# A graph network on one core: sixteen small products of each batch dealt out among its columns

## The chip, the cores and the metric

One NeuronCore of a Trainium2 chip runs the whole program in one launch. The metric is the device time in microseconds, the median over the runs. The core has a matrix engine (TensorE; PE in the rows, its weight loads PEld), VectorE (DVE), ScalarE (ACT), GpSimd (POOL) and SyncE (SP), each with its own instruction stream; they meet only at semaphores.

## The reference, cut to what matters

The program is a chain of four graph layers over 3,750 nodes and 123,750 edges (`src`, `dst`, with attributes): a relational convolution, a weighted one, two attention layers and a tensor product. All of them sum messages per destination node:

```
msg = Hr[src, etype] * norm
agg = jax.ops.segment_sum(msg, dst, num_segments=N)
```

The kernel sorts the edges by destination once, so that every later layer walks them in that order. The change lies in this sort.

## The kernel before, in words

The sort has two parts. `count_edges` counts the edges of each node and so finds each node's first free slot. `place_edges` then takes the edges in 121 batches (`SBATCHES`) of 8 columns (`SB`) of 128 edges, finds for each edge the slot that it goes to, and GpSimd scatters the 80-byte records to DRAM, one indirect DMA for each column (line 717).

A destination is split in a low part (7 bits, `lo`) and a high part (`hi`, 30 values, `BLKS`). A table of counters over (low, high) is a 128 x 30 array. An edge's slot is the sum of three things, all summed by TensorE into `own[j][:, k, 0:BLKS]` for batch buffer `j` (the batch's number modulo 2) and column `k`:

- `earlier` x `hot_hi` (line 667): edges of the same column that stand earlier and go to the same node;
- `hot_lo_t` x `taken_in` (line 671): what the earlier columns of the batch have taken. `taken[j]` counts it (line 673, a product of the one-hots `hot_lo` and `hot_hi` that adds up over the columns, its end raises `added`), and ScalarE copies it as f16 to `taken_in` after each column but the last (line 704, raises `taken_copied`);
- `hot_lo_t` x `high` and `hot_lo_t` x `low` (lines 677 to 682, the rows call them L680): the nodes' next free slots at the start of the batch, as two f16 digits. These are 2 x 8 = 16 products of 128x128 by 128x30. They stand behind the eighth column, in one burst; ahead of them is a wait on `based`, and the last raises `owned`.

VectorE, for each batch `b` in this order: `find_base(b)` waits for all `added` of batch b-1, adds `taken` to the base and splits it into `high` and `low` (lines 612 to 615, the last raises `based`); `pick_slots(b-1)` waits for `owned` of batch b-1, picks the slot of each edge (lines 620 to 624) and makes row numbers (lines 232 to 235, the last raises `rows_ready`); `find_hots(b+1)` makes the one-hots of the next batch (lines 596 to 601, the last raises `hot`). TensorE begins batch b after `hot` of batch b. GpSimd waits for `rows_ready` of a batch and sends its 8 indirect DMAs. The one-hots, `own` and `taken` have two buffers, `rows` four.

Beside this, 240 chunks of the first layer's table are made: up to two for each batch, a 128x128 by 128x512 f32 product behind the columns 2 and 5 (line 656), copied out by ScalarE (line 695) and stored by SyncE. SyncE also loads `lo_wide`, 256 KB for each batch (line 571), as soon as `hot` frees its buffer.

Of the kernel before, what the change touches and what calls it, by code (L numbers as in the profile page):

```python
# [31 lines left out]
BLKS = -(-N // P)  # L32
# [10 lines left out]
SB = 8  # L43
# [201 lines left out]
def sort_edges(env, inp, dst, records, relation_layers, weights_dram, table):  # L245

    nc = env.nc
    with ExitStack() as ctx:
        sb, ps = stage_memory(nc, ctx, "sort")
        parts = {
            "recs": sb("recs", [P, EC, REC], F32),
            "lo": sb("lo", [P, EC], F16),
            "hi": sb("hi", [P, EC], F16),
            "lo_f32": sb("lo_f32", [P, EC], F32),
            "node_row": sb("node_row", [P, BLKS], I32),
            "node_rec": sb("node_rec", [P, BLKS, REC], F32),  # L260
            "base": sb("base", [P, 2, BLKS], F32),
            "space": sb("space", [P, D * D // 2], F32),
        }
        lo_rows = nc.dram_tensor("lo_rows", (EC, P), F16, kind="Internal").ap()
        count_edges(env, inp, dst, records, relation_layers, weights_dram, lo_rows, parts)
        place_edges(env, records, lo_rows, table, parts)
# [249 lines left out]
def place_edges(env, records, lo_rows, table, parts):  # L516
# [14 lines left out]
    with ExitStack() as ctx:  # L531
# [3 lines left out]
        hot_lo_t = sb("hot_lo_t", [P, 2, SB, P], F16)  # L535
        earlier = sb("earlier", [P, 2, SB, P], F16)
        hot_hi = sb("hot_hi", [P, 2, SB, BLKS], F16)
        high = sb("high", [P, 2, BLKS], F16)
        low = sb("low", [P, 2, BLKS], F16)
# [9 lines left out]
        own = [ps(f"own{j}", [P, SB, 64], F32) for j in range(2)]  # L549
# [4 lines left out]
        s = {n: env.sig(f"place_{n}").sem for n in (  # L554
            "hot", "based", "added", "taken_copied", "owned", "rows_ready", "self_written", "x_turned", "x_ready",
            "table_made", "table_out")}
# [3 lines left out]
        table_rows = table.rearrange("(n h r) f -> n h (r f)", h=2, r=REL // 2)  # L560
        block = ctx.enter_context(nc.Block(no_gpsimd_drain=True))

        def table_chunks(b):
            return range(max(0, (b - made_at) * per_batch), min(BLKS * chunks, (b - made_at + 1) * per_batch))

        @block.sync
        def _(sp):
            def load_lo(b):
                if b >= lo_bufs:
                    sp.wait_ge(s["hot"], b - lo_bufs + 1)  # L570
                sp.dma_start(lo_wide[:, b % lo_bufs, :, :].rearrange("p k e -> p (k e)"),
                             lo_rows[b * SB:(b + 1) * SB, :].rearrange("k e -> (k e)").partition_broadcast(P)
                             ).then_inc(lo_in[b % lo_bufs], 16)

            def store(half):
                sp.wait_ge(s["table_out"], 4 * half + 4)
                sp.dma_start(table_rows[half // 2 * P:(half // 2 + 1) * P, half % 2, :], made[half % 3]).then_inc(stored[half % 3], 16)

            half = 0
            for b in range(SBATCHES):  # L580
                load_lo(b)
                while half < halves and 4 * half + 4 <= max(0, (b - lo_bufs - made_at) * per_batch):
                    store(half)
                    half += 1
            for last in range(half, halves):
                store(last)
            for j in range(3):
                sp.wait_ge(stored[j], 16 * len(range(j, halves, 3)))
# [54 lines left out]
        @block.tensor  # L643
        def _(pe):
            def turn_x(blk):
                if blk:
                    pe.wait_ge(s["x_ready"], blk)
                pe.transpose(turn_ps[:, 0:P], env.x[:, blk, :], env.ident[:, :]).then_inc(s["x_turned"], 1)

            def make_table(n):  # L650
                blk, c = n // chunks, n % chunks
                if c == 0:
                    pe.wait_ge(s["x_ready"], blk + 1)
                if n >= 2:
                    pe.wait_ge(s["table_out"], n - 1)
                pe.matmul(out_ps[n % 2][:, :], x_t[:, blk % 2, :], weights[:, c * cols:(c + 1) * cols], start=True,
                          stop=True).then_inc(s["table_made"], 1)
                if c == 0 and blk + 1 < BLKS:
                    turn_x(blk + 1)

            turn_x(0)
            for b in range(SBATCHES):
                j = b % 2
                left = list(table_chunks(b))
                pe.wait_ge(s["hot"], b + 1)
                for k in range(SB):
                    pe.matmul(own[j][:, k, 0:BLKS], earlier[:, j, k, :], hot_hi[:, j, k, :], start=k == 0, stop=True,
                              skip_group_check=True)
                    if k:
                        pe.wait_ge(s["taken_copied"], b * (SB - 1) + k)  # L670
                        pe.matmul(own[j][:, k, 0:BLKS], hot_lo_t[:, j, k, :], taken_in[:, k % 2, :], start=False, stop=True,  # L671
                                  skip_group_check=True)
                    pe.matmul(taken[j][:, 0:BLKS], hot_lo[:, j, k, :], hot_hi[:, j, k, :], start=k == 0, stop=True,
                              skip_group_check=True).then_inc(s["added"], 1)
                    if left and k in (2, 5):
                        make_table(left.pop(0))
                pe.wait_ge(s["based"], b + 1)
                for k in range(SB):
                    for digit in (high, low):
                        mm = pe.matmul(own[j][:, k, 0:BLKS], hot_lo_t[:, j, k, :], digit[:, j, :], start=False, stop=True,  # L680
                                       skip_group_check=True)
                mm.then_inc(s["owned"], 1)

        @block.scalar
        def _(act):
# [1864 lines left out]
```

## Time and profile before

| what | value |
|---|---|
| median of 3 runs | 11323.88 us (11316.15 to 11333.89) |
| the profiled execution, its time | 11423.42 us |
| its span, first to last instruction | 11421.7 us |
| mean granted TensorE clock | 0.623 of full speed |
| PE / PEld / DVE / ACT / POOL busy | 62% / 46% / 51% / 27% / 58% of the span |
| indirect DMAs of the placing stage (line 717) | 968, from 166.3 to 1681.8 us |

The profiled execution is one run with the profiler on; its time stands above the median of the plain runs. Shares are means over stages with different limits, so they don't say what the placing stage waits for. In the rows below a start is in microseconds from the first instruction; "idle before" is the time in which that engine did nothing ahead of the instruction, with what released it. A PE row's start is when the product was issued to the array; when it was done shows in the instruction that waits for its semaphore.

### The profile page before, as it was taken

What the parts mean: (1) busy time and instruction counts of PE and PEld (TensorE: products, weight loads), DVE (VectorE), ACT (ScalarE), POOL (GpSimd) and SP (SyncE); (2) the same over time, 40 slices, a digit from 0 to 9 for tenths busy, and PEclk for the clock granted to TensorE, in tenths of its full rate; (3) what the DMA queues carried; (4) which work ended last, traced back from release to release, by engine and by line L of the source; (5) the groups of instructions that cost most, each with busy time, mean ns of one, the idle gap of its engine ahead of it and who ended that gap; (6) DMA issues with size and microseconds to landing.
All of it is one profiled execution on the core that took longest, in us unless ns stands there. A gap on an engine that the chain in (4) does not pass through costs nothing. (4 is left out here: it accounts for less than half of the span.)

```text
span 11421.7 us, 173435 instructions
## 1 busy us (share of the span) xinstructions
PE 7099.6 (62%) x35190; PEld 5300.1 (46%) x35190; DVE 5879.9 (51%) x20916; ACT 3126.7 (27%) x10511; POOL 6581.8 (58%) x6970
## 2 busy tenths in 40 slices
PE   5444444433383333358888767777577777788888
PEld 3222223333332323334444356666566666777777
DVE  5555543333333333345544456666566666677776
ACT  2111110000020000000000044444344444677776
POOL 3666666666515655656666566666466665455554
PEclk5555555555585555555555556666666656899999
DMA  3222223111151111111111111111111111211111
GB/s 99 72 69 69 72 73 80 46 45 44 42 227 44 44 44 42 44 45 46 46 46 45 45 48 49 49 48 49 44 48 48 48 48 43 75 41 41 41 41 40
DMA packets 312728, 637.47 MB, mean 56 GB/s; under 512 B 138402, under 2 KB 181541, under 8 KB 300200
## 3 DMA queue, kind: packets, MB, share of 16 engines
q0 software_dynamic: 222080, 416.54, 14.1%
q1 hardware_dynamic: 81444, 212.40, 5.4%
q14 instruction: 579, 4.74, 0.1%
q8 instruction: 141, 2.31, 0.1%
q10 hardware_dynamic: 8484, 1.48, 0.1%
HBM read 479.02 MB, written 150.90 MB: 55 GB/s over the span
## 5 line engine op out<-in xcount | busy, mean ns | idle before, releaser
L1185 POOL DMA_INDIRECT relsum_rows<-relation_table,tab_idx x1950 | 1842.2, 945 | 1422.7 <-issue 484.9
L1241 PE MATMUL relsum_sums<-relsum_hot,relsum_rows 128*128 128x128 f32 x3900 | 1109.3, 449 | 1452.5 <-issue 797.1
L1241 PEld LDWEIGHTS relsum_sums<-relsum_hot,relsum_rows 128*128 128x128 f32 x3900 | 915.6, 307 | 1638.9 <-issue 1600.7
L1053 POOL DMA_INDIRECT conv_rows<-tensor_table,src_idx x997 | 939.9, 943 | 750.9 <-PE conv_sums L2360 357.2
L1053 POOL DMA_INDIRECT gat2sum_rows<-gat_table,src_idx x997 | 942.8, 946 | 587.7 <-PE gat2sum_sums L1971 308.6
L1053 POOL DMA_INDIRECT gat1sum_rows<-gat_table,src_idx x997 | 941.6, 944 | 582.3 <-PE gat1sum_sums L1971 255.1
L717 POOL DMA_INDIRECT records<-sort_recs,place_rows x968 | 926.4, 957 | 595.0 <-DVE place_rows L235 325.1
L1185 POOL DMA_INDIRECT gcnsum_rows<-x_table,src_idx x985 | 935.0, 949 | 562.6 <-PE gcnsum_sums L1241 259.1
L1969 PE MATMUL gat1sum_sums<-gat1sum_hot,gat1sum_scaled 128*128 128x128 f32 x1994 | 686.1, 443 | 413.0 <-DVE gat1sum_scaled L1898 332.9
L1197 DVE TENSOR_SCALAR relsum_hot<-iota_row,dst_rel,w 128x128 f32<-128x128 f32 x1994 | 722.8, 365 | 423.5 <-issue 421.4
L1969 PE MATMUL gat2sum_sums<-gat2sum_hot,gat2sum_scaled 128*128 128x128 f32 x1994 | 671.5, 436 | 432.3 <-DVE gat2sum_scaled L1898 302.0
L1241 PE MATMUL gcnsum_sums<-gcnsum_hot,gcnsum_rows 128*128 128x128 f32 x1970 | 781.9, 500 | 0.0
L2238 ACT ACTIVATE conv_rows_attr<-conv_rows,conv_rec 128x64 f32<-128x64 f32 x2991 | 737.8, 333 | 13.4 <-SPq L2197 12.8
L1969 PEld LDWEIGHTS gat2sum_sums<-gat2sum_hot,gat2sum_scaled 128*128 128x128 f32 x1994 | 469.3, 291 | 565.4 <-issue 509.7
L1969 PEld LDWEIGHTS gat1sum_sums<-gat1sum_hot,gat1sum_scaled 128*128 128x128 f32 x1994 | 470.3, 292 | 555.9 <-DVE gat1sum_scaled L1898 429.9
L1218 DVE TENSOR_TENSOR acc<-acc,relsum_sums 128x128 f32 x997 | 287.4, 288 | 823.7 <-PE relsum_sums L1241 376.5
L1240 PE MATMUL gcnsum_sums<-gcnsum_hot,ones 128*1 128x128 f32 x1994 | 581.1, 394 | 199.7 <-issue 139.3
L1218 DVE TENSOR_TENSOR acc<-acc,gcnsum_sums 128x256 f32 x997 | 419.6, 421 | 553.4 <-PE gcnsum_sums L1241 515.8
L671 PE MATMUL place_own<-place_taken_in,place_hot_lo_t 128*128 128x30 f16 x847 | 170.4, 201 | 841.5 <-ACT place_taken_in L704 675.5
L1241 PEld LDWEIGHTS gcnsum_sums<-gcnsum_hot,gcnsum_rows 128*128 128x128 f32 x1970 | 492.5, 310 | 421.2 <-issue 421.2
L1218 DVE TENSOR_TENSOR rel_acc<-rel_acc,relsum_sums 128x128 f32 x997 | 287.2, 288 | 725.3 <-remote 462.8
L2283 DVE TENSOR_TENSOR tp_acc<-tp_acc,conv_sums 128x384 f32 x999 | 550.0, 551 | 170.6 <-PE conv_sums L2360 119.0
(410 smaller groups left out, 15931.9 us busy)
## 6 DMA issues: line engine op xcount, KB each, us to landing
relation_table<-table_row SPq DMA_DIRECT2D x30, 2048.0 KB, 6.3
relsum_rows_SP<-relation_table SPq DMA_DIRECT2D x2816, 0.5 KB
relsum_rows_ACT<-relation_table ACTq DMA_DIRECT2D x2816, 0.5 KB
relation_table<-sort_space SPq DMA_DIRECT2D x40, 1024.0 KB
relsum_rows<-relation_table,tab_idx POOLq DMA_INDIRECT x1950
place_lo_wide<-lo_rows SPq DMA_DIRECT2D x121, 256.0 KB
gcnsum_rows_SP<-x_table SPq DMA_DIRECT2D x1536, 0.5 KB
relation_table<-place_extra SPq DMA_DIRECT2D x20, 1024.0 KB
```

Source lines behind the costliest of these rows:

```text
L671: pe.matmul(own[j][:, k, 0:BLKS], hot_lo_t[:, j, k, :], taken_in[:, k % 2, :], start=False, stop=True, skip_group_check=True)
L717: pool.indirect_dma_start(records, bass.IndirectOffsetOnAxis(ap=rows[:, b % row_bufs, k:k + 1], axis=0), recs[:, b * SB + k, :], None).the ...
L1053: pool.indirect_dma_start(bufs[:, t % depth, :], None, table, bass.IndirectOffsetOnAxis(ap=idx[:, t:t + 1], axis=0)).then_inc(landed[t % l ...
L1185: pool.indirect_dma_start(rows[:, t % depth, :], None, table, bass.IndirectOffsetOnAxis(ap=idx[:, t:t + 1], axis=0)).then_inc(landed[t % d ...
L1197: dve.tensor_scalar(hot[:, t % HOTS, :], env.iota_row[:, :], env.dst_rel[:, t:t + 1], weight[:, t:t + 1], ALU.is_equal, ALU.mult).then_inc ...
L1218: dve.tensor_tensor(window, window, sums[t % banks][:, 0:parts * P].rearrange("p (a n) -> p a n", a=parts), ALU.add).then_inc(s["added"], 1)
L1240: pe.matmul(bank[0:1, P:2 * P], env.ones[:, 0:1], hot[:, t % HOTS, :], start=True, stop=True)
L1241: pe.matmul(bank[:, 0:P], tile_rows, hot[:, t % HOTS, :], start=True, stop=True).then_inc(s["multiplied"], 1)
L1969: pe.matmul(bank[:, 0, 0:P], scaled[:, j, :, :].rearrange("p h c -> p (h c)"), hot[:, k, :], start=True, stop=True)
L2238: last = act.activation(rows_attr[:, k % 8, m, :].rearrange("p (i u) -> p i u", i=2), by_block[:, 0:m + 2:m + 1, :], ACT.Identity, scale=a ...
L2283: dve.tensor_tensor(window, window, sums[(k - 2) % 4][:, 0:3 * P].rearrange("p (a n) -> p a n", a=3), ALU.add).then_inc(s["added"], 1)
```

## The change

The burst behind the eighth column goes. Behind column `k` TensorE now sends the digit products of the columns in `based_after[k]`: none behind 0 and 1, four behind column 2 (for the columns 0 and 1), two behind each of 3, 4, 5 and 6 (for the columns 2, 3, 4 and 5), four behind column 7 (for the columns 6 and 7). There are 16 as before, on the same operands. The wait on `based` moves from behind column 7 to behind column 2's `taken` product. Behind the columns 2 and 5 they stand ahead of the table's chunk. Only TensorE's stream is touched.

```
+        BASED_AT = 2
+        based_after = [(), (), (0, 1), (2,), (3,), (4,), (5,), (6, 7)]
...
                     pe.matmul(taken[j][:, 0:BLKS], hot_lo[:, j, k, :], hot_hi[:, j, k, :], start=k == 0, stop=True,
                               skip_group_check=True).then_inc(s["added"], 1)
+                    if k == BASED_AT:
+                        pe.wait_ge(s["based"], b + 1)
+                    for done in based_after[k]:
+                        for digit in (high, low):
+                            mm = pe.matmul(own[j][:, done, 0:BLKS], hot_lo_t[:, j, done, :], digit[:, j, :], start=False,
+                                           stop=True, skip_group_check=True)
+                    if k == SB - 1:
+                        mm.then_inc(s["owned"], 1)
                     if left and k in (2, 5):
                         make_table(left.pop(0))
-                pe.wait_ge(s["based"], b + 1)
-                for k in range(SB):
-                    for digit in (high, low):
-                        mm = pe.matmul(own[j][:, k, 0:BLKS], hot_lo_t[:, j, k, :], digit[:, j, :], start=False, stop=True,
-                                       skip_group_check=True)
-                mm.then_inc(s["owned"], 1)
```

## Rows read from the trace of the kernel before

**Rows 1.** The page's first part, and the granted clock in 40 slices.

```profile
span 11421.7 us, 173435 instructions
...
PEclk5555555555585555555555556666666656899999
```

**Rows 2.** Placing stage by windows: us, PE, PEld, DVE, ACT, POOL busy (x), PEclk, DMA, GB/s.

```profile
129.00:1682.00 1553.00, 698.07 (x5228) 342.36 (x5228) 783.72 (x2410) 278.12 (x1116) 950.37 (x994) 0.50 0.21 68
```

**Rows 3.** Tiles picked and rows: durations ns min/median/max, first and last start; last, waits.

```profile
L620 DVE TENSOR_TENSOR place_picked<-place_own,place_hot_hi x121: 399/408/409, 164.3 to 1669.3; 128x240 f32<-128x240 f32 x121
...
L717 POOL DMA_INDIRECT records<-sort_recs,place_rows  x968: 952/958/987, 166.3 to 1681.8; - x194
...
  DVE place_rows L235: 325.1, 111
```

**Rows 4.** Timeline of one batch: start, duration, instruction, idle before and its releaser.

```profile
829.22 0.21 PE L671 MATMUL place_own<-place_taken_in,place_hot_lo_t 128*128 128x30 f16 x1 [5.62 <-ACT place_taken_in L704]
...
829.53 0.96 POOL L717 DMA_INDIRECT records<-sort_recs,place_rows  x1 [2.14 <-DVE place_rows L235]
829.73 0.20 PE L671 MATMUL place_own<-place_taken_in,place_hot_lo_t 128*128 128x30 f16 x1 [0.25 <-ACT place_taken_in L704]
...
836.08 0.19 PE L673 MATMUL place_taken<-place_hot_hi,place_hot_lo 128*128 128x30 f16 x1
...
836.11 0.19 PE L680 MATMUL place_own<-place_high,place_hot_lo_t 128*128 128x30 f16 x1
...
836.30 0.19 DVE L612 TENSOR_TENSOR sort_base<-place_taken,sort_base 128x30 f32<-128x30 f32 x1 [2.41 <-PE place_taken L673]
...
836.51 0.19 PE L680 MATMUL place_own<-place_low,place_hot_lo_t 128*128 128x30 f16 x1
...
836.66 0.19 DVE L615 TENSOR_TENSOR place_low<-sort_base,place_high 128x30 f16<-128x30 f32 x1
...
838.37 0.95 POOL L717 DMA_INDIRECT records<-sort_recs,place_rows  x1 [0.30 <-issue]
840.20 0.41 DVE L620 TENSOR_TENSOR place_picked<-place_own,place_hot_hi 128x240 f32<-128x240 f32 x1 [3.35 <-issue]
...
840.93 0.18 ACT L704 CAST place_taken_in<-place_taken 128x30 f16<-128x30 f32 x1 [4.95 <-remote]
...
842.18 0.95 POOL L717 DMA_INDIRECT records<-sort_recs,place_rows  x1 [2.86 <-DVE place_rows L235]
```

**Rows 5.** Timeline of the first batch, GpSimd scattering the nodes' own records beside it.

```profile
139.03 0.19 DVE L612 TENSOR_TENSOR sort_base<-place_taken,sort_base 128x30 f32<-128x30 f32 x1 [4.87 <-remote]
...
160.23 1.10 POOL L712 DMA_INDIRECT records<-sort_node_rec,sort_node_row  x1 [0.30 <-issue]
164.28 0.41 DVE L620 TENSOR_TENSOR place_picked<-place_own,place_hot_hi 128x240 f32<-128x240 f32 x1 [24.70 <-remote]
```

**Rows 6.** Timeline of two batches, where GpSimd went from one to the next unbroken.

```profile
797.76 0.19 PE L680 MATMUL place_own<-place_low,place_hot_lo_t 128*128 128x30 f16 x1
...
799.85 0.41 DVE L620 TENSOR_TENSOR place_picked<-place_own,place_hot_hi 128x240 f32<-128x240 f32 x1 [1.71 <-remote]
...
802.69 0.18 ACT L704 CAST place_taken_in<-place_taken 128x30 f16<-128x30 f32 x1 [2.62 <-remote]
...
813.41 0.18 ACT L704 CAST place_taken_in<-place_taken 128x30 f16<-128x30 f32 x1 [2.68 <-remote]
...
815.34 0.19 PE L680 MATMUL place_own<-place_low,place_hot_lo_t 128*128 128x30 f16 x1
...
817.58 0.96 POOL L717 DMA_INDIRECT records<-sort_recs,place_rows  x1 [5.89 <-DVE place_rows L235]
...
823.33 0.19 PE L680 MATMUL place_own<-place_low,place_hot_lo_t 128*128 128x30 f16 x1
```

**Rows 7.** Timeline of the last batch, VectorE with no further batch to prepare.

```profile
1668.47 0.19 PE L680 MATMUL place_own<-place_low,place_hot_lo_t 128*128 128x30 f16 x1
...
1669.32 0.41 DVE L620 TENSOR_TENSOR place_picked<-place_own,place_hot_hi 128x240 f32<-128x240 f32 x1 [6.71 <-PE place_own L680]
```

## The prediction

> **What bounds the kernel now.** I read the page first, for where the time lies, then the placing stage by windows, then the lists of the tiles `picked` and `rows`, and at last the timelines of single batches, since a mean over the stage hides what alternates in it.
>
> The change touches one stage. The stage runs from 129 to 1682 us, 1,553 us of a span of 11,421.7 [rows 1, 2], 13.6% of it. TensorE's clock is at 0.50 there, its lower level of 1.2 GHz, in each of the six slices that it spans [rows 1, 2], and nothing in the change gives it more work, so the clock stays out of the sum. No engine fills the stage: GpSimd is busy for 950 of 1,553 us, VectorE 784, TensorE 698 [rows 2]. It is bound by a loop of waits.
>
> The loop's period: VectorE's `place_picked` stands 121 times from 164.3 to 1669.3 us [rows 3], so a batch takes 1505.0/120 = 12.54 us. In the batch shown [rows 4], GpSimd starts its eight scatters at 829.53 and the eighth at 838.37, 1.263 us apart; it ends at 839.32, idles 2.86 us and starts again at 842.18. GpSimd waits for the row numbers (325.1 us over 111 waits [rows 3]). They wait for the pick, the pick for `owned`. The pick starts at 840.20 and leads to the scatter 1.98 us later: VectorE's short chain, untouched by the change.
>
> Why is `owned` so late? TensorE issued the last of the 16 products at 836.51, and the pick started 3.69 us later with VectorE idle [rows 4]. ScalarE's copy of the next batch's first column came at 840.93 though its product follows right behind. So products were issued on time and were done late. Both were released around the end of GpSimd's scatters (839.32): `owned` 0.88 us after it, the copy 1.61 us after it. Three other stretches say the same. In the first batch GpSimd sends indirect DMAs without a pause; its last starts at 160.23, and only at 164.28 does the pick come, for the 16 products behind column 7, while VectorE had read the count from before them at 139.03 [rows 5]: 25.2 us for 16 products, 1.58 each. With GpSimd idle the burst costs nothing: issued by 815.34, scatters from 817.58 after 5.89 us idle, so the pick lay about 2 us before that [rows 6, 4]. And in the last batch, with no further one-hots to make, the burst is done 0.85 us after its last issue though GpSimd is busy [rows 7]. I read it so: while GpSimd works for several microseconds on end, products finish at a low rate, and a backlog of them is let go when it pauses. What in the chip does this no row tells.
>
> **The change, part by part.** *Removed*: 16 products issued from 836.11 to 836.51, 15 gaps of 26.7 ns [rows 4], behind column 7. *Added*: the same 16, 12 of them behind columns 2 to 6. Between a column's products and the next column's, TensorE idles 0.25 us (829.73 [rows 4]) waiting for ScalarE's copy; two products take 0.05 us and four take 0.11, so they hide in that gap, and the columns keep their pace. If that cover is gone, because the products ahead of a column are done late, each column waits for them too. What is left behind column 7 is 4 products, so `owned` could come 12 x 26.7 ns = 0.32 us earlier, and the next batch's first column too. *Table chunks* behind the columns 2 and 5 start 0.11 and 0.05 us later, beside two microseconds of their own work: nothing. *DMAs*: none is moved; SP and GpSimd have the same queues.
>
> *The moved wait.* Behind `based` at column 2 now stand all later columns, ScalarE's copies, and through `added` VectorE. `based` is done at 836.66 + 0.19 = 836.85, 0.77 us after the issue of column 7's `taken` at 836.08 [rows 4]. The next batch's column 2 cannot be there sooner than two column steps after its first (829.22 to 829.73 is one, 0.51 us), so 1.02 us after a first column issued 0.16 us behind that `taken`: 1.18 us against 0.77. 0.41 us to spare, and 4 us more in a batch like that of [rows 4]. Cost nothing; were the spare gone, it would be at most 0.77 us x 120 = 92 us.
>
> *The sum.* On paper 0.32 us x 120 = 38 us are to be had (0.3% of the span). But `owned` is not let go by its own issue: it follows the end of GpSimd's scatters. In [rows 4] it had 3.69 us of lateness, and an issue 0.32 us sooner adds to the lateness only. So the likeliest sum is zero: 11,423.4 for a profiled execution. That run stands 99.5 us above the median of the plain runs; taken as the same on both sides, the median is to be 11,323.9 less a few microseconds for the batches in which GpSimd idles and the burst is in the open. I say 11,320, its own range 11,300 to 11,345.
>
> At this place a page speaks. The Trainium skill ("SBUF — State Buffer", section "SBUF: two separate sides") says that on the engine side only VectorE and GpSimd get in each other's way, and TensorE never waits on anyone. By that the burst would cost its issue and no more, and the gain would be the paper's 38 us. The trace does not show that freedom: with GpSimd busy the pick came 3.69 us late, with it idle it did not.
>
> **The rivals.**
>
> *Faster: the issue counts after all.* The 0.32 us pass on to the period: 11,324 - 38 = 11,285. More if the smaller tail lets `owned` go one step sooner: in [rows 4] the two releases are 0.73 us apart, and 0.73 x 120 = 88 us gives 11,236. For it speaks that the last batch's 16 products got through in 1.25 us from first issue (1669.32 against 1668.47 - 0.40) with GpSimd busy [rows 7], so four may pass where sixteen don't. The floor is GpSimd without a pause, 8 x 1.263 = 10.10 us a batch: (12.54 - 10.10) x 120 = 293 us, 11,031. I hold that to be out of reach, since unbroken scatters are just what slows TensorE [rows 5, 6]. The skill's rule above comes out here, at 11,285.
>
> *Slower: `owned` early, GpSimd unbroken, the columns starve.* This is the same premise with its sequel. In [rows 6] `owned` came 1.71 us after VectorE had gone idle, early enough that GpSimd went on without a break. The next batch's columns then crawled (ScalarE idled 2.62 us between two copies at 802.69, where in [rows 4] a whole column takes 0.51 us), and its last product was issued 815.34 - 797.76 = 17.58 us after the one before, against 823.33 - 815.34 = 7.99 us for the batch after GpSimd's pause. The pair took 25.57 us, 12.79 a batch: 0.25 us more than the mean. If the change turns this into the rule, that is 120 x 0.25 = 30 us, 11,354. And it is worse after the change: from 797.8 to the copy of the sixth column at 813.41 [rows 6] GpSimd kept TensorE slow, 15.6 us in which two products of the first column and three of each of the next five were finished, 17 in all, 0.92 us each. Now 10 of about as many would be digit products, so three columns fewer are done, and each is made up for at 0.97 us ((836.08 - 829.27)/7): 3.2 us, less the 0.32 saved. A pair of 28.5 us is 14.2 a batch: 120 x 1.7 = 204 us, 11,528. It decides from the point at which four products behind column 7 get through while GpSimd is on its fifth or sixth scatter. For it: two or three products do (column 7's `taken` at 836.08 is seen by VectorE at 836.30 with GpSimd busy). Against it: the rate that a busy GpSimd leaves may depend on the sum of products, and that is the same.
>
> *The wait on `based`*, 92 us at most, has 0.41 us to spare; I give it no case of its own.
>
> **How the numbers follow.** A change within 0.2% (23 us) is about what a measurement of this kernel can't tell from none. Same, 0.41: nothing but lateness is moved. Slower, 0.33: the starving columns, from 11,354 to 11,528. Faster, 0.26: 11,285 or 11,236, the latter with a third of it. The forecast is the first. The range of 8 in 10 takes in both rivals' first values and most of the way to the slower one's far end: 11,230 to 11,500; about 1 in 10 is left on each side (a floor towards 11,031 below, the full price of 11,528 above).
>
> **What would show it.** In the trace after: the digit products stand between the columns with gaps of 0.03 us, four behind column 7; the 0.25 us gaps ahead of the columns stay or shrink by nothing. If I am right, the period from pick to pick is 12.4 to 12.7 us, the pick comes within 1.7 us of the end of GpSimd's eighth scatter, and GpSimd idles 2 to 4 us between batches. If the slower rival is, GpSimd's pauses come every second batch and are 5 us or longer, and copies at the columns 1 to 5 come 1 to 3 us late. If the faster one is, the period falls below 12.35 with the pauses evenly shorter. I am wrong most simply if the profiler makes the lateness: the plain runs would then not be bound by it, and the period that I read is not theirs; the 99.5 us between the two bound this at 0.8 us a batch.

## The result and the profile after

The kernel after took 11,517.39 us (median of three runs, 11,497.68 to 11,519.37) against 11,323.88 before: a ratio of 1.0165, 95% interval 1.0142 to 1.0188, so 194 us slower. The forecast was 11,320.

The page of the kernel after, its first line and the granted clock in 40 slices:

```profile
span 11495.8 us, 173435 instructions
...
PEclk5555555555567555555555566666666566899999
```

The placing stage by windows, columns as in [rows 2]:

```profile
129.00:1887.00 1758.00, 702.66 (x5228) 340.15 (x5228) 781.56 (x2413) 285.44 (x1116) 954.28 (x994) 0.50 0.19 60
```

The tiles picked and rows, columns as in [rows 3]:

```profile
L624 DVE TENSOR_TENSOR place_picked<-place_own,place_hot_hi x121: 399/401/408, 157.7 to 1872.8; 128x240 f32<-128x240 f32 x121
```

```profile
L723 POOL DMA_INDIRECT records<-sort_recs,place_rows x968: 955/962/992, 162.2 to 1886.5; - x194
...
  DVE place_rows L235: 519.4, 60
```

The busy times of all engines are those of [rows 2] within 8 us, and the clock is at the same level, 0.50. The stage is 205 us longer (last scatter at 1886.5, was 1681.8 [rows 3]), all of it idle time. From pick to pick it is (1872.8 - 157.7)/120 = 14.29 us, was 12.54. And the wait row tells how: GpSimd waited for rows 60 times, 8.7 us each, where in [rows 3] it waited 111 times, 2.9 us each. Every second pause is gone and the other one has trebled. That the profiled span grew by 74 us only lies in the other stages of the profiled run of before: behind its last scatter it took 9,739.9 us, against 9,609.3 here. The late experiments below that scatter beside the batches fall into the same two groups: their spans behind the last scatter are 9,591 to 9,628 us on two chips, and 9,739 and 9,749 us on a third, which also has the kernel before at 11,445; so that run of before may have been on such a chip, which nothing here can show.

Two batches of the kernel after, timeline, columns as in [rows 4]:

```profile
751.96 0.40 DVE L624 TENSOR_TENSOR place_picked<-place_own,place_hot_hi 128x240 f32<-128x240 f32 x1
753.93 0.96 POOL L723 DMA_INDIRECT records<-sort_recs,place_rows  x1 [9.05 <-DVE place_rows L235]
756.18 0.18 ACT L710 CAST place_taken_in<-place_taken 128x30 f16<-128x30 f32 x1 [0.33 <-issue]
...
759.01 0.19 PE L683 MATMUL place_own<-place_low,place_hot_lo_t 128*128 128x30 f16 x1
759.60 0.40 DVE L624 TENSOR_TENSOR place_picked<-place_own,place_hot_hi 128x240 f32<-128x240 f32 x1
760.24 0.18 ACT L710 CAST place_taken_in<-place_taken 128x30 f16<-128x30 f32 x1 [1.44 <-PE place_taken L677]
763.08 0.18 ACT L710 CAST place_taken_in<-place_taken 128x30 f16<-128x30 f32 x1 [2.66 <-remote]
763.37 0.19 PE L677 MATMUL place_taken<-place_hot_hi,place_hot_lo 128*128 128x30 f16 x1
764.05 0.96 POOL L723 DMA_INDIRECT records<-sort_recs,place_rows  x1 [0.30 <-issue]
765.22 0.18 ACT L710 CAST place_taken_in<-place_taken 128x30 f16<-128x30 f32 x1 [1.95 <-remote]
765.50 0.19 PE L677 MATMUL place_taken<-place_hot_hi,place_hot_lo 128*128 128x30 f16 x1
770.88 0.59 ACT L701 COPY sort_space<-place_out 128x512 f32<-128x512 f32 x1 [5.47 <-remote]
772.91 0.96 POOL L723 DMA_INDIRECT records<-sort_recs,place_rows  x1 [0.30 <-issue]
774.37 0.18 ACT L710 CAST place_taken_in<-place_taken 128x30 f16<-128x30 f32 x1 [2.91 <-remote]
...
779.91 0.19 PE L671 MATMUL place_own<-place_hot_hi,place_earlier 128*128 128x30 f16 x1
780.42 0.40 DVE L624 TENSOR_TENSOR place_picked<-place_own,place_hot_hi 128x240 f32<-128x240 f32 x1
782.39 0.96 POOL L723 DMA_INDIRECT records<-sort_recs,place_rows  x1 [8.53 <-DVE place_rows L235]
```

Read it from GpSimd's start at 753.93. The last of the four products behind column 7 is issued at 759.01 and the pick comes at 759.60, when GpSimd is on its fifth scatter. So the next rows are ready while it works, and at 764.05 it goes on without a break (0.30 us is its gap between any two scatters). From there the columns crawl: column 3's `taken` is issued at 765.50 and copied at 774.37, half a microsecond after GpSimd's sixteenth scatter has ended (772.91 + 0.96). Between the copies of columns 2 and 3 (765.22 and 774.37) nine products were finished: four digit products behind column 2, the table chunk's two, and the three of column 3; 9.15 us, 1.02 us each. Columns 4 to 7 follow in 5.4 us once GpSimd is idle, which it is for 8.53 us. The next pair goes the same way. `based` (ready at 759.7 for that batch) was waited for nowhere.

This batch is typical. From GpSimd's start behind a pause to the next pick it takes 5.67 us (the median of 60 pauses); before it took 10.61 (the median of 115). The next rows come 2 us behind the pick, and GpSimd's eight scatters last 9.8 us: now the rows are there before it has ended, before they weren't.

### The profile page after: what moved, and what is told of

Its sections match the earlier page's. It is cut to its first block and busy times, and to the rows that moved or that the text cites. A ratio compares the mean times of both kernels' runs of the same rounds, so it can differ in the third digit from the quotient of the medians.

```text
span 11495.8 us, 173435 instructions
## 1 busy us (share of the span) xinstructions
PE 7059.6 (61%) x35190; PEld 5266.7 (46%) x35190; DVE 5872.5 (51%) x20916; ACT 3133.6 (27%) x10511; POOL 6600.6 (57%) x6970
## 5 line engine op out<-in xcount | busy, mean ns | idle before, releaser
L675 PEld LDWEIGHTS place_own<-place_taken_in,place_hot_lo_t 128*128 128x128 f16 x847 | 97.7, 115 | 1260.4 <-ACT place_taken_in L710 780.0
```

## The experiments

**Two conditions.** The runs fell into two conditions of the chip, those measured together always in the same one. In one, called late here, the kernel before takes 11,297 to 11,324 us (11,445 on one chip), and TensorE's products are finished late beside GpSimd's scatters. In the other, on time, it takes 9,373 to 9,375 us, and no copy of `taken` in the stage comes more than 0.63 us behind the issue of its product. That lag is the measure of lateness below: a copy is called late where it is over 0.7 us. Of the 839 copies from 160 us on (all but the first batch's), 165 are late in the trace of before and 261 in that of after. One chip showed both, twenty minutes apart. Nothing in a kernel chooses it. The forecast, the result and the profiles of before and after are of the late one.

### On time: the change and no lateness

`after_again` and `before_again` are the two kernels unchanged.

> The kernel after, unchanged, measured again beside the kernel before. In the last set of runs the kernel before took 9,373 us, not 11,324, and in no profiled execution there was a product of TensorE done late under GpSimd's scatters: GpSimd sent all its batches without a pause, 10.1 us each, and set the stage's end. Theory G with that: where products are not done late, the change has nothing to make worse and nothing to gain, since GpSimd without a pause is the stage's bound; ratio 1.000 within 0.001, GpSimd's pauses 0.3 us, every copy 0.2 to 0.6 us behind its product. If this set shows the lateness (kernel before near 11,320), the ratio is 1.014 to 1.019 again and the batches alternate. Rival B (the dealt products have a price of their own, whatever GpSimd does): slower by 1.5% or more in either condition.

> The kernel before, unchanged, profiled in the same set as the kernel after. Theory G: near 9,370 us and GpSimd unbroken from the second batch on, with the pick done well ahead of the scatters; or, where products are done late, 12.5 us a batch as in the trace of before. The 2,000 us between the two conditions should then lie wherever GpSimd sends indirect DMAs beside TensorE's work, in all stages that do so, and not in this stage alone.

Measured: after 9,375.24, before 9,374.79, ratio 1.0001 (0.9992 to 1.0010). From the kernel before in this condition, its page and its tile picked:

```profile
span 9376.3 us, 173435 instructions
...
L1185 POOL DMA_INDIRECT relsum_rows<-relation_table,tab_idx x1950 | 1847.6, 947 | 825.2 <-issue 453.0
...
L717 POOL DMA_INDIRECT records<-sort_recs,place_rows x968 | 926.8, 957 | 295.2 <-issue 295.2
```

```profile
L620 DVE TENSOR_TENSOR place_picked<-place_own,place_hot_hi x121: 393/400/408, 135.4 to 1337.7; 128x240 f32<-128x240 f32 x121
```

GpSimd's 295.2 us of idle time are its 968 gaps of 0.30 us; it waits for rows nowhere, and its eight scatters take 10.10 us, the floor of the prediction. (The picks run ahead of it by up to four batches of rows, so from first to last pick it is (1337.7 - 135.4)/120 = 10.02 us.) The first batch's pick comes at 135.4, not at 164.28 [rows 5], with GpSimd scattering beside it all the same. The 2,000 us between the conditions lie where GpSimd sends such DMAs beside TensorE: its idle time ahead of them, summed over the six stages that do so, is 2,037 us more on the page of the kernel before than here, and the spans differ by 2,045. In the stage with the largest part it idles 825.2 us here, and in the late condition, on the page of the kernel before,

```profile
L1185 POOL DMA_INDIRECT relsum_rows<-relation_table,tab_idx x1950 | 1842.2, 945 | 1422.7 <-issue 484.9
```

with the same 0.95 us for one issue. The change does nothing here because GpSimd sets the pace in both kernels.

`last_after` and `last_before` take GpSimd off the loop:

```diff
-        rows = sb("rows", [P, row_bufs, SB], I32)
+        rows = sb("rows", [P, SBATCHES, SB], I32)
...
-                if b >= row_bufs:
-                    dve.wait_ge(scattered[b % row_bufs], 16 * SB * (b // row_bufs))
...
+            pool.wait_ge(s["rows_ready"], SBATCHES)
             for b in range(SBATCHES):
-                pool.wait_ge(s["rows_ready"], b + 1)
```

> The kernel after, with the rows of all 121 batches kept and the 968 scatters sent only when the last batch's rows are there, so that GpSimd is idle while TensorE works. Theory G (TensorE's products are done late only while GpSimd sends indirect DMAs without a break): every batch goes like the quick ones of the trace after, 7.64 us from pick to pick instead of 14.29, no copy by ScalarE more than 0.3 us behind its product, and the scatters follow at 1.263 us each (1,223 us). Rival B (the columns themselves became long, by the digit products in them or by the wait on `based`): the period stays well above that of the same edit on the kernel before, by 1.5 us or more.

> The kernel before with the same edit (all scatters behind the last batch). Theory G: 7.9 to 8.0 us from pick to pick instead of 12.54 (the batch after GpSimd's pause in the trace of before had 7.99), the 16 products in the open at 27 ns each, so 0.3 us a batch more than the kernel after under the same edit: the change's paper gain of 0.32 us shows here. Rival B: this one is faster than the kernel after under the same edit.

Measured, one run each: 10,267.69 and 10,286.95 us, 7.68 and 7.85 us from pick to pick ((1056.6 - 135.1)/120 and (1077.0 - 135.1)/120). With no scatter beside it the dealing saves 0.17 us a batch, half of the 0.32 us on paper: the eight columns, from the first `taken` to the last, take 7.48 us in most batches with the dealt products and 7.33 without. The 0.15 us lie behind the two table chunks, which start later: the column behind the first comes 0.10 us later and the one behind the second 0.05. Rival B, a larger price of the columns' own, is out.

`tail8` leaves eight products behind column 7, and `gate7` makes GpSimd wait for TensorE's column 7 of the next batch:

```diff
-        based_after = [(), (), (0, 1), (2,), (3,), (4,), (5,), (6, 7)]
+        based_after = [(), (), (0,), (1,), (2,), (3,), (), (4, 5, 6, 7)]
```

```diff
                 pool.wait_ge(s["rows_ready"], b + 1)
+                if b + 1 < SBATCHES:
+                    pool.wait_ge(s["added"], (b + 1) * SB + 8)
```

> Between the two kernels: 8 digit products are left behind column 7, not 4 or 16; the other 8 stand behind columns 2 to 5, one node's pair each. Theory G, if what decides is whether the tail gets through before GpSimd stops: either the alternation of the kernel after (14.2 us a batch, 11,500 us) or the even period of before (12.5 us, 11,320), with few batches of a third kind; I lean to the alternation at 0.6, for 8 products at about 0.9 us each are 7.2 us and GpSimd's batch has 9.8. Rival B (each product dealt among the columns has its price): 8 of 12 dealt products give 8/12 of 1.75 us, so 13.7 us a batch and 11,450 us, with no alternation.

> The kernel after, and GpSimd sends the scatters of a batch only when TensorE has also finished column 7 of the next batch. Theory G: TensorE's columns then run while GpSimd is idle or has just begun, so GpSimd pauses in every batch by a little, the alternation is gone, and the period falls to 9.8 us of scatters and 0.6 to 1.7 us of pause, 10.4 to 11.5 us: 11,070 to 11,200 us, faster than both kernels. Rival B: GpSimd begins later in each batch and nothing gets quicker: 14.3 us a batch or more, 11,520 us or above. Rival C (the products are late by the scatters' traffic and not by the breaks in it): columns crawl under each batch of scatters all the same, and the period is about 9.8 us and a tail of 5 us or more.

Measured: 9,372.56 and 9,374.76 us against 9,372.73 (0.9999 and 1.0001, each within 0.001). Neither expectation was tested, as no product was late; both were measured again below.

### Late: where the lateness comes from

`last_after_late` is `last_after` again.

> The same kernel as in the run last_after (all scatters behind the last batch), anew for the same reason. Where products are late: by theory G they are late only beside GpSimd's indirect DMAs, so the period is 7.68 us as before and no copy comes more than 0.65 us behind its product; by a rival in which TensorE itself is slow in this condition, 8.5 us or more.

Measured: 11,937.88 us; period 7.74 us ((1087.5 - 158.5)/120), 0.06 us above the one on time, and one late copy of 839, at 166 us, the start of the stage. TensorE is not slow in this condition by itself; it is slow beside GpSimd's scatters. `fill` goes one further: scatters still last, but GpSimd fills a scratch tile beside the batches.

```diff
             for b in range(SBATCHES):
                 pool.wait_ge(s["rows_ready"], b + 1)
+                for part in range(8):
+                    pool.memset(rest[:, :], 0.0).then_inc(s["rested"], 1)
+                    pool.wait_ge(s["rested"], 8 * b + part + 1)
+            for b in range(SBATCHES):
```

> All scatters behind the last batch as in last_after, and beside the batches GpSimd fills a scratch tile eight times a batch (about 8.2 us), with no DMA of its own. If it is GpSimd's DMAs that make TensorE late, the copies come 0.22 to 0.65 us behind their products as in last_after and the period is GpSimd's own, 8 to 9 us, or 7.7. If any work of GpSimd's does it, columns crawl and the period is 10 us or more. VectorE may lose some time to GpSimd's fills, both being on the same tiles' side of the memory; that would show as longer instructions, not as late ones.

Measured: 11,914.96 us. The tiles picked and rest:

```profile
L625 DVE TENSOR_TENSOR place_picked<-place_own,place_hot_hi x121: 399/401/408, 158.5 to 1090.8; 128x240 f32<-128x240 f32 x121
```

```profile
L722 POOL MEMSET place_rest<- x968: 847/847/887, 162.6 to 1100.0; 128x900 f32 x194
```

GpSimd works 6.8 us of each 7.77 us batch and nothing crawls (one late copy again, at 167 us). Its waits for rows are 0.57 us on average (68.6 us over 120), shorter than the 0.72 us that turns out below to be too short a break between scatters. So it is the indirect DMAs, not a busy GpSimd. `half_after` and `half_before` send four of a batch's scatters beside the batches and the other four at the end:

```diff
-            for b in range(SBATCHES):
-                pool.wait_ge(s["rows_ready"], b + 1)
-                for k in range(SB):
...
+            for late in (False, True):
+                for b in range(SBATCHES):
+                    if not late:
+                        pool.wait_ge(s["rows_ready"], b + 1)
+                    for k in range(SB // 2, SB) if late else range(SB // 2):
```

> The kernel after, in which GpSimd sends only the first four scatters of a batch beside the batches (5.05 us of its time) and the other four of every batch behind the last one (484 x 1.263 = 611 us more at the end). GpSimd is then no bound in any condition and is never busy for more than 5 us on end. Where TensorE's products are on time (kernel before near 9,373 us): theory G expects the columns to set the period, 7.68 us as with all scatters behind the batches, and 0.17 us less than the same edit on the kernel before. Where they are late (kernel before near 11,320): G expects little lateness, since breaks of 2.5 us or more come in every batch, a period of 7.7 to 9 us and no alternation; a rival by which each scatter costs TensorE its share, break or none, expects 10 us or more, with columns that crawl under the four scatters.

> The kernel before with the same edit. On time: 7.85 us from pick to pick, so 0.17 us x 120 = 20 us slower than the kernel after with it (0.2%). Late: by G a period of 8 to 9.3 us; the 16 products fall under the scatters of the batch before or just behind them, whichever comes first.

Measured: 11,331.22 and 11,338.58 us against 11,297.39 (1.0032 and 1.0043, their intervals overlap). GpSimd in `half_after`, timeline:

```profile
481.89 0.96 POOL L723 DMA_INDIRECT records<-sort_recs,place_rows  x1 [0.30 <-issue]
486.24 0.96 POOL L723 DMA_INDIRECT records<-sort_recs,place_rows  x1 [3.39 <-DVE place_rows L235]
487.51 0.96 POOL L723 DMA_INDIRECT records<-sort_recs,place_rows  x1 [0.30 <-issue]
488.77 0.96 POOL L723 DMA_INDIRECT records<-sort_recs,place_rows  x1 [0.30 <-issue]
490.04 0.96 POOL L723 DMA_INDIRECT records<-sort_recs,place_rows  x1 [0.31 <-issue]
```

Periods 7.93 and 7.97 us: with never more than 4.8 us of scatters on end and some 3 us of break, hardly a product is late: 3 copies of 839 in `half_after` and 2 in `half_before`, all but one of them at the start of the stage. A price per scatter, break or none, is out too.

### Late: the number of products behind column 7

> The same kernel as in the run tail8 (8 digit products behind column 7), anew for the same reason. Where products are late, theory G leans to the alternation of the kernel after (14.2 us a batch, some 11,500 us, at 0.6), else the even 12.5 us of before; rival B expects 13.7 us a batch with no alternation, 11,450 us.

Measured: 11,493.07 us against 11,298.97, ratio 1.0166 (1.0149 to 1.0184).

```profile
L624 DVE TENSOR_TENSOR place_picked<-place_own,place_hot_hi x121: 400/407/409, 161.0 to 1877.9; 128x240 f32<-128x240 f32 x121
```

```profile
  DVE place_rows L235: 526.2, 60
```

14.31 us a batch in full alternation, as the kernel after with 12 dealt products. Not a price for each product dealt, which would have made 13.7 us. Eight products behind column 7 get through in time. In the timelines of this run and of the kernel before:

```profile
756.89 0.95 POOL L723 DMA_INDIRECT records<-sort_recs,place_rows  x1 [9.09 <-DVE place_rows L235]
763.97 0.41 DVE L624 TENSOR_TENSOR place_picked<-place_own,place_hot_hi 128x240 f32<-128x240 f32 x1 [1.28 <-remote]
```

```profile
827.55 0.41 DVE L620 TENSOR_TENSOR place_picked<-place_own,place_hot_hi 128x240 f32<-128x240 f32 x1 [3.88 <-remote]
```

In three batches column 7's `taken` is issued at about the same point of GpSimd's stretch, 5.0 to 5.3 us behind its start: at 758.91 in the trace after, at 761.91 here, and at 822.90 in the batch of [rows 6] in which GpSimd starts at 817.58. With 4 digit products behind it the pick comes 5.67 us behind GpSimd's start, with 8 it comes at 7.08, with 16 at 9.97. One batch does not fit: in the last one of the kernel before [rows 7] GpSimd starts at 1662.88, and all 16 are through by 1669.32, after 6.44 us. VectorE then has no further batch to prepare and TensorE none to begin; which of these lets them through, no run shows.

`gate3` is `gate7` with `(b + 1) * SB + 4`.

> The same kernel as in the run gate7 (GpSimd sends a batch's scatters only when TensorE has finished column 7 of the next batch), measured anew, since the last set of runs had the late products again (kernel before 11,297 us) which the set with gate7 had not. Where they are late, theory G expects what was expected of gate7: a pause of GpSimd in every batch, no alternation, 10.4 to 11.5 us a batch, 11,050 to 11,180 us. Rival B: 14.3 us a batch and 11,500 us. Rival C: 12 to 15 us, with columns that crawl under every batch of scatters.

> The kernel after, and GpSimd sends a batch's scatters only when TensorE has finished column 3 of the next batch: a weaker gate. Where products are late, theory G expects TensorE to have column 3 of the next batch done under the first 7.5 us of the scatters in the good case, and so unbroken pairs again with a smaller loss: 11.5 to 13.5 us a batch, 11,180 to 11,430 us. Rival C expects it as slow as gate7.

Measured: `gate7` 11,467.74 us, 1.0145 (1.0128 to 1.0162); `gate3` 11,305.38 us, 1.0004 (0.9994 to 1.0014). The first misses its expectation. In its trace, GpSimd's starts:

```profile
742.05 0.96 POOL L725 DMA_INDIRECT records<-sort_recs,place_rows  x1 [0.30 <-issue]
743.31 0.96 POOL L725 DMA_INDIRECT records<-sort_recs,place_rows  x1 [0.30 <-PE place_taken L677]
744.58 0.96 POOL L725 DMA_INDIRECT records<-sort_recs,place_rows  x1 [0.31 <-issue]
...
753.42 0.96 POOL L725 DMA_INDIRECT records<-sort_recs,place_rows  x1 [0.30 <-issue]
762.32 0.96 POOL L725 DMA_INDIRECT records<-sort_recs,place_rows  x1 [7.95 <-PE place_taken L677]
```

The next batch begins at 744.58 without a pause, so its gate was open: in the long pause TensorE is ahead and gets through the next batch's eight columns in the first part of GpSimd's. A gate on TensorE's progress forces no break where TensorE is ahead; it moves the pairs by a batch. The earlier gate, `gate3`, has 12.59 us a batch, about what the kernel before has (12.54). The sum for `gate7` took a pause in every batch for granted. `gate3` came out within what was expected of it.

### Late: breaks between the scatters

`rest1` has GpSimd fill a scratch tile twice behind the eighth scatter; `rest2` once behind the fourth and once behind the eighth:

```diff
                                             recs[:, b * SB + k, :], None).then_inc(scattered[b % row_bufs], 16)
+                    if k in (3, 7):
+                        pool.memset(rest[:, :], 0.0).then_inc(s["rested"], 1)
+                        pool.wait_ge(s["rested"], 2 * b + k // 4 + 1)
```

> The kernel after, and GpSimd fills a scratch tile twice behind every eighth scatter (two fills of 900 columns, about 1.0 us each by the fill of 600 columns that took 0.68), so that it sends no DMA for some 2.3 us after each batch. Where products are late: if a break in the DMAs once a batch is what lets them go, the alternation is gone and the period is 10.1 + 2.1 = 12.2 us, 250 us less than the kernel after and some 40 us less than before: 11,250 us. If 2.3 us is too short a break, pairs remain and the period is 14.3 us and more. Where products are on time (before near 9,373): 12.2 against 10.1 us a batch, 9,620 us.

> The same total rest in two pieces, one fill of about 1.0 us behind the fourth and one behind the eighth scatter, so that DMAs are never sent for more than 5 us on end, but with breaks of only some 1.3 us. Late: if it is the length of the unbroken stretch that makes products late, 12.2 us a batch and hardly any lateness; if it is the length of the break that lets them go (at least 1.6 us by the trace of before), products stay late and the period is well above that of rest1, 13.5 us or more. On time: the same 9,620 us.

Measured: 11,233.46 and 11,207.88 us against 11,298.92: 0.9937 (0.9921 to 0.9954) and 0.9915 (0.9899 to 0.9932). Both beat the kernel before; by the ratios to it they are 2.2 and 2.5% below the kernel after. GpSimd in `rest2`, timeline, and what the rows' scatters waited for:

```profile
654.22 0.96 POOL L724 DMA_INDIRECT records<-sort_recs,place_rows  x1 [0.30 <-issue]
655.17 0.86 POOL L727 MEMSET place_rest<- 128x900 f32 x1
656.31 0.96 POOL L724 DMA_INDIRECT records<-sort_recs,place_rows  x1 [0.28 <-POOL place_rest L727]
```

```profile
L724 POOL DMA_INDIRECT records<-sort_recs,place_rows x968: 954/958/992, 161.9 to 1597.6; - x194
...
  DVE place_rows L235: 11.2, 1
```

A break of 1.14 us between two DMAs (655.17 to 656.31) after each four scatters, or one of 2.05 after each eight, and GpSimd waits for rows once in the whole stage. It sets the pace, at 11.8 us a batch. It does more (242 fills of 0.86 us) and the stage is 84 us shorter than before (last scatter 1597.6 against 1681.8 [rows 3]). By the trace of before I had taken 1.6 us as the break that lets products go; 1.14 does. The two breaks don't do the same, though. In `rest2` 17 copies of 839 are late; in `rest1` 228 are, and the time is won because the backlog goes before GpSimd has run out of rows.

`extra` doubles each of the 12 dealt products, the copy into columns that nobody reads:

```diff
+                            if k < SB - 1:
+                                pe.matmul(own[j][:, done, 32:32 + BLKS], hot_lo_t[:, j, done, :], digit[:, j, :], start=False,
+                                          stop=True, skip_group_check=True)
                             mm = pe.matmul(own[j][:, done, 0:BLKS], hot_lo_t[:, j, done, :], digit[:, j, :], start=False,
```

> The kernel after, and each of the 12 dealt digit products stands twice, the copy adding into columns that nobody reads. Late: if a busy GpSimd leaves TensorE a fixed number of products (17 in the starved batch of the trace after), the starved batch gets through one column less before GpSimd stops, 0.5 to 1.0 us more per pair of batches, so 30 to 60 us more than the kernel after in all: 11,520 to 11,560 us. If each product had its price of 0.9 us in every batch, 12 x 0.9 x 120 = 1,300 us more. On time: no difference from 9,373, GpSimd is the bound.

Measured: 11,530.94 us, 1.0202 (1.0185 to 1.0219), period 14.39 us ((1894.8 - 168.1)/120). Twelve more products a batch cost 0.1 us of period, not 11. I read it so, without a run that shows it: what the batch gets through while it starves is set by GpSimd's stretch, and the rest is made up in the pause.

`rest_short` is `rest2` with fills of 400 columns instead of 900; `rest_before` is the kernel before with the rests of `rest2`.

> As rest2, with fills of 400 columns (about 0.4 us instead of 0.86) behind the fourth and the eighth scatter. Where products are late: if a break of 0.7 us between two DMAs is enough, GpSimd sets the period at 10.1 + 0.9 = 11.0 us and the kernel takes 11,207 - 0.8 x 120 = 11,110 us; if it is too short, TensorE falls behind GpSimd, which then waits for rows, and the time is above 11,207 us, up to the 11,500 of the pairs. I give the first 0.4. On time (before near 9,373): 0.9 us x 120 = 105 us slower than before.

> The kernel before (all 16 products behind column 7) with the rests of rest2. Where products are late: if the breaks are all that is needed, GpSimd sets the pace here too and the time is that of rest2, 11,208 us within 0.2%, so that dealing out the products is worth nothing even then; if the 16 products in a burst still wait for a break each time, the period is longer than rest2's, 12 to 12.5 us, 11,230 to 11,290 us.

Measured, on a chip where the kernel before takes 11,445.04 us: 11,454.98 (1.0009, 1.0000 to 1.0018) and 11,352.28 (0.9923, 0.9910 to 0.9937). `rest_short`:

```profile
L724 POOL DMA_INDIRECT records<-sort_recs,place_rows x968: 954/958/987, 165.3 to 1705.1; - x194
...
  DVE place_rows L235: 224.8, 63
  POOL place_rest L727: 26.6, 96
```

Its fills take 0.45 us, its breaks 0.72 (the fill and its 0.28 us), and GpSimd waits for rows 63 times again; 359 of 839 copies are late. It takes back the loss of the change (1.0009 where the kernel after had 1.0165) but gains nothing. So for stretches of four scatters the break that is enough lies between 0.72 and 1.14 us. And `rest_before` gains what `rest2` gains, the intervals overlap: once the breaks are there, where the 16 products stand makes no difference to the time (126 copies are late, and GpSimd waits for rows twice).

## Why the prediction was wrong, by its own steps

*What bounds the kernel* held: the loop of waits, products issued on time and finished late beside GpSimd. The 0.92 us each that was read off [rows 6] left out the table chunk's two products behind column 2; with them it is 19 in 15.6 us, 0.82 each. In the trace after it is 17 in 15.4 us, 0.90 each (759.01 to 774.37). `last_after_late`, `fill` and `half_after` show that it is GpSimd's indirect DMAs, sent without a break, beside which it happens.

*The step that failed* is in the sum: "`owned` is not let go by its own issue: it follows the end of GpSimd's scatters", so that an earlier issue "adds to the lateness only". That was read from a batch with 16 products behind column 7 and taken over to 4. Four got through 5.67 us behind GpSimd's start and eight 7.08 (`tail8_late`), on its fifth and sixth scatter, where 16 took 10.61 by the median. The last batch [rows 7] got 16 through by 6.44 us, so their number is not all that counts; but the three batches set side by side above, with `taken` issued at the same point, come in the order of it.

*What took its place* is the slower rival, in mechanism and in size. Its condition, four products through while GpSimd is on its fifth or sixth scatter, is met in the trace after (759.60 against the start at 753.93); its pair of 28.5 us is 28.6 (2 x 14.29); its 120 x 1.7 = 204 us are 120 x 1.75 = 210, and 194 in the median. The forecast gave it 0.33. What it was given as evidence against, that the rate may depend on the sum of products, falls with the result: the sum is the same and the time is not. And its evidence for stood in [rows 6]: the batch whose `owned` came early was followed by the unbroken stretch. The last batch [rows 7], read as support for the faster rival, speaks as well for this one, since an early `owned` is what starts the starving.

That its size came out so close is in part luck. The sum put 10 digit products among 17 and so three columns fewer. In the trace after, 4 of the 17 are digit products and 2 the chunk's, and four columns are copied where six were, two fewer. What grew is GpSimd's long pause, from 5.89 us [rows 6] to 8.53, 2.6 us where the sum had 2.9. And `extra` put four more products ahead of column 3 and lengthened the pair by 0.2 us, where 0.5 to 1.0 was expected.

*The faster rival's* floor, GpSimd without a pause, is the on-time condition's normal state (10.10 us a batch), in both kernels; there the change is worth nothing. Its 0.32 us a batch is 0.17 where nothing else binds (`last_before` against `last_after`).

*The wait on `based`*: no cost, as said. *The table chunks*: costed at nothing; in the open their later start takes back 0.15 of the 0.32 us a batch (`last_after` against `last_before`), and in a starved batch their two products queue with the rest at about 1 us each, before and after alike. *The profiler as the cause of the lateness* is not excluded. The prediction bounded it by the 99.5 us between the profiled run and the plain ones. But each plain run here comes with a recorded span and granted clock as well, so none of them is known to have gone without recording.

What stays open is what makes the chip late in one condition and not in the other, and whether GpSimd's issuing of the DMAs or their traffic is what TensorE meets: no run parts the two. The traces show no difference in the stage's clock, in the packets moved or in the duration of GpSimd's issues. They do show that it is not TensorE alone: SyncE's 4,395 register moves take 29 ns each on time (`before_again`), and 209 ns on average late (`before`), one in six of them 0.7 us or more.

And the recording itself differs. The same 173,435 instructions leave 162,457 records of semaphore updates in the trace of `before_again` and 51,604 in that of `before`. They are missing where products are late. From 166 to 600 us the first has 6,508 updates by DMAs and the second 1,255; in `last_after` and `last_after_late`, with no scatters there, it is 1,366 and 1,333, and from 1,300 to 1,680 us, with scatters and nothing beside them, 4,816 in both. So a third rival stands untested: that the path of the records is full in the late condition and holds TensorE up. It may as well suffer from the same cause. Only a run without any recording could tell, and with it whether the change costs anything outside of a recorded run.

The Trainium skill ("SBUF — State Buffer", section "SBUF: two separate sides") has TensorE never wait on another engine at that memory's engine ports. On time nothing in the trace speaks against it: copies come 0.22 to 0.63 us behind their products with GpSimd unbroken. In the late condition column 3's product is copied 8.9 us behind its issue; whether it waited at a port, no row shows, and the harmless `fill`, in which GpSimd writes that memory for 6.8 us of each batch, speaks against it.

## What to carry to other kernels

Where a wait comes back late, ask what the waiting engine does when it comes back early: here a producer's pause was what let the other engine work, and a shorter chain took every second pause away. A pause that looks like loss can be the cheap one; 1.1 us of deliberate rest for GpSimd after every four indirect DMAs bought 0.8% where the change lost 1.65%. Where the lateness is absent it should cost some 200 us, by the floor of 10.10 us against 11.8 a batch (worked out, not run), so measure the kernel before beside every variant, at the same time on the same chip.

## What the runs showed of the hardware that was not expected

- The same kernel takes 9,375 or 11,300 us, on the same chip at different times, with the same clock in the stage (0.50) and the same 0.95 us for each indirect DMA's issue. The slower condition's trace has a third of the faster one's records of semaphore updates (51,604 against 162,457).
- In the late condition TensorE's products finish at about one in 1.0 us beside GpSimd's indirect DMAs sent on end (9 in 9.15 us), in the trace after from some 6 us behind GpSimd's start. Beside fills that keep GpSimd busy for 6.8 of each 7.77 us they are on time.
- A break of 1.14 us after each four indirect DMAs leaves 17 of 839 copies late; one of 2.05 us after each eight leaves 228, and GpSimd still waits for rows only once. A break of 0.72 us after each four leaves 359.
